# Turning x for the later batches on VectorE and through DRAM, unit-matrix transposes ahead of the first input, and a reordered end of the attention

## What is computed

```python
B, LQ, LK, D, H, HD = 4, 512, 512, 512, 16, 32
x = layer_norm(hidden_states, ln1_w, ln1_b)
q = (x @ q_w + q_b)                      # heads of 32
k = (encoder_hidden_states @ k_w + k_b)
v = (encoder_hidden_states @ v_w + v_b)
scores = where(mask, q k^T / sqrt(32), lowest)
out = softmax(scores) v
hidden = out @ cproj_w + cproj_b + hidden_states
y = layer_norm(hidden, ln2_w, ln2_b)
return hidden + gelu(y @ fc_w + fc_b) @ proj_w + proj_b   # inner width 2048
```

## Time and profile before

| | |
|---|---|
| median of 3 runs | 778.49 us (778.36 to 780.44) |
| profiled execution | 777.89 us, of which the span of the profile is 776.0 us |
| PE busy | 746.5 us, 96% |
| DVE, ACT, POOL busy | 468.8, 281.0, 276.9 us |
| projections | until about 152 us |
| attention | until about 410 us |
| MLP | until the end |

### The profile page before, as it was taken

The page is one execution under the profiler, slowest core; times in us unless marked ns, Lnnn a source line. Parts: engine busy times, 40 slices in busy tenths (PEclk is TensorE's granted clock), DMA queues, the critical chain, the costliest instruction groups (busy, mean ns, idle before and its releaser), DMA issues.

```text
span 776.0 us, 10021 instructions
## 1 busy us (share of the span) xinstructions
PE 746.5 (96%) x3664; PEld 514.7 (66%) x3664; DVE 468.8 (60%) x1012; ACT 281.0 (36%) x492; POOL 276.9 (36%) x166
## 2 busy tenths in 40 slices
PE   6999999889899999999979999999999999999998
PEld 5878886633334434444436888888888888888886
DVE  6673346889988899999768577533423343232213
ACT  3434241276766666667764011111112111211110
POOL 2654150066877677788644002113002200230000
PEclk9999999999999999999999999999999999999999
DMA  9656377587656785578640538240220404030001
GB/s 325 228 167 221 132 225 235 183 252 175 159 126 161 186 221 152 151 203 182 176 135 28 190 97 207 91 161 2 41 68 1 163 14 96 1 108 1 1 0 55
DMA packets 94384, 103.24 MB, mean 133 GB/s; under 512 B 39968, under 2 KB 48420, under 8 KB 94336
## 3 DMA queue, kind: packets, MB, share of 16 engines
q1 hardware_dynamic: 94192, 102.59, 45.5%
q10 hardware_dynamic: 144, 0.02, 0.0%
HBM read 73.08 MB, written 29.37 MB: 132 GB/s over the span
## 4 chain that ended last, share of the span: by engine, by line
PE 72%; DVE 19%; issue 3%; DMA 2%; ACT 2%; SPq 1%; POOL 0%; DVEq 0%; ACTq 0%
PE ps L481 20%; PE ps L483 20%; PE ps L482 20%; DVE ps L1001 10%; PE ps L604 3%; PE ps L573 3%; PE ps L588 3%; DVE R L1128 2%; PE ps L619 2%; DVE mx L1001 1%; PE ps L541 1%; DVE R L1022 1%; ACT Pt L790 1%; DMA RAWY<-in_q_w 1%; DVE R L937 1%
## 5 line engine op out<-in xcount | busy, mean ns | idle before, releaser
L790 ACT ACTIVATE Pt<-ps 128x512 f32<-128x512 f32 x256 | 137.4, 597 | 75.3 <-PE ps L588 74.1
L1175 DVE CAST HR<-R 128x512 fp32r<-128x512 f32 x52 | 24.3, 468 | 185.3 <-ACT R L825 185.3
L825 ACT ACTIVATE R<-ps,cols 128x512 f32<-128x512 f32 x52 | 35.9, 690 | 227.2 <-PE ps L483 227.1
L588 PE MATMUL ps<-BIG 98*128 98x512 f32 x256 | 93.4, 442 | 7.3 <-DVE R L1006 3.4
L1001 DVE CUSTOM_DVE_ANT_0 ps<-ps,FU 128x512 f32<-128x512 f32 x128 | 84.4, 720 | 14.5 <-PE ps L573 14.4
L588 PEld LDWEIGHTS ps<-BIG 98*128 98x128 f32 x256 | 44.8, 190 | 72.3 <-issue 24.6
L1001 DVE CUSTOM_DVE_ANT_0 ps<-ps,BIG 128x512 f32<-128x512 f32 x128 | 84.3, 720 | 7.6 <-PE ps L573 7.6
L481 PE MATMUL ps<-BIG,HR 128*128 128x512 f32 x192 | 74.8, 390 | 0.7 <-DVE HR L1177 0.7
L481 PE MATMUL ps<-YT,BIG 128*128 128x512 f32 x192 | 75.0, 390 | 0.0
L482 PE MATMUL ps<-YT,BIG 128*128 128x512 f32 x192 | 74.8, 389 | 0.0
L483 PE MATMUL ps<-BIG,HR 128*128 128x512 f32 x192 | 74.7, 389 | 0.0
(11 more groups left out here) (131 smaller groups left out, 1368.6 us busy)
## 6 DMA issues: line engine op xcount, KB each, us to landing
BIG<-qs SPq DMA_DIRECT2D x62, 256.0 KB, 2.7
BIG<-ks SPq DMA_DIRECT2D x62, 256.0 KB, 3.2
ks<-BIG SPq DMA_DIRECT2D x32, 256.0 KB, 2.1
qs<-BIG SPq DMA_DIRECT2D x32, 256.0 KB, 5.6
R<-hd SPq DMA_DIRECT2D x28, 256.0 KB, 4.4
R<-in_x SPq DMA_DIRECT2D x16, 256.0 KB, 5.5
hd<-R SPq DMA_DIRECT2D x16, 256.0 KB, 3.1
yt<-FU SPq DMA_DIRECT2D x64, 64.0 KB, 2.0
```

The lines of the kernel that those rows point to most:

```text
L588: eng.matmul(bk, K_[0:98, j, kc * 128:(kc + 1) * 128], Q_[0:98, j, :], start=True, stop=True).then_inc(S["p_ra"], 1)
L790: eng.activation(Pt[:, r, j % 2, :], bank(bank_a(("s2", i, j))), ACT.Exp, scale=SCALE).then_inc(S["a_ra"], 1)
L825: eng.activation(g, bank(4 + i % 2), ACT.Gelu_apprx_tanh, bias=fcb[:, f:f + 1]).then_inc(S["a_g"], 1)
L1175: eng.tensor_copy(HR[:, n, 0, :], g).then_inc(S["v_hh"], 1)
```

## The change

1. PE runs 16 transposes of the unit matrix by itself as soon as it is there, before its first projection. Nothing reads their result.
2. Only x of batch 0 is still turned by PE. For batches 1 to 3 DVE turns the normalized tile in 32x32 blocks (`x_block`, four STREAM_TRANSPOSE) into a buffer in the place of the high part of x, SP stores the blocks to `yt` in 16 DMAs of 64 KB in runs of 32 elements (`x_store`), loads them back in four DMAs (`x_load`) into R2, and `x_affine` works in place there and waits for the loads. The block transposes stand directly behind `x_norm`, ahead of the next group of low parts (L988) on DVE. On ACT `x_high(1)` stands behind the first V eviction of batch 1. On POOL the roots for batches 2 and 3 stand ahead of `x_low(1)` and behind `x_low(2)`. DMAs for raw x and for the leads wait for the block transposes instead of PE's.
3. At the end of the attention the affine, high and low parts of the second layer norm stand two items later, and `divide_c(12)` one item earlier, ahead of the pair adds.

```diff
-        Y_NORM, Y_BLOCKS, Y_AFFINE = (45, 47, 49, 51), (48, 49, 52, 53), (56, 56, 56, 56)
-        Y_HIGH, Y_LOW = (57, 57, 58, 58), (58, 58, 59, 59)
+        Y_NORM, Y_BLOCKS, Y_AFFINE = (45, 47, 49, 51), (48, 49, 52, 53), (58, 58, 58, 58)
+        Y_HIGH, Y_LOW = (59, 59, 60, 60), (60, 60, 61, 61)
...
+            def x_store(b):
+                dst = yt[b].rearrange("(k i) (c q j) -> c q i k j", i=32, q=4, j=32)
+                for c in range(4):
+                    sp.wait_ge("v_xb", 4 * (b - 1) + c + 1)
+                    for q in range(4):
+                        eng.dma_start(dst[c, q], blocks(b, c)[32 * q:32 * q + 32].rearrange(
+                            "i (k j) -> i k j", j=32)).then_inc(S[f"d_xs{c}"], 16)
+
+            def x_load(b):
+                sp.wait_ge("g_xl", 4 * b)
+                for c in range(4):
+                    sp.wait_ge(f"d_xs{c}", 64 * b)
+                for k in range(4):
+                    eng.dma_start(R2[:, k, :], yt[b, 128 * k:128 * k + 128]).then_inc(S[f"d_xl{k}"], 16)
...
             for b in range(B):
                 if b == 3:
                     load_stack(1)
+                if 0 < b < 3:
+                    x_store(b + 1)
                 for g in range(4):
                     store_qk(b, g, 0)
+                    if 0 < b < 3 and g == 1:
+                        x_load(b + 1)
...
                     load_raw(3, cv[2], 2)
+                    x_store(1)
...
                     if b == 0 and g == 1:
                         sp.wait_ge("g_lo", 3)
                         load_raw(0, xv[2], 2)
+                    if b == 0 and g == 2:
+                        x_load(1)
...
+            pe.wait_ge("cst", 2)
+            for n in range(16):
+                eng.transpose(bank(n % 4)[:, 0:128], ident[:, :], ident[:, :])
...
-                if 0 < b < 3:
-                    x_turn(b + 1)
...
-                    if b == 0 and g == 3:
-                        x_turn(1)
...
                     act.wait_ge("p_pj", 12 * b + c + 1)
                     eng.activation(V[:, 4 * b + c, :], bank(proj_bank(12 * b + c)), ACT.Copy).then_inc(S["a_v"], 1)
+                    if b == 1 and c == 0:
+                        x_high(1)
...
-                    if b == 0 and g == 3:
-                        x_high(1)
...
+            def x_block(b):
+                i = RAW_X[b][0]
+                if b >= 2:
+                    dve.wait_ge("p_pj", 12 * (b - 2) + 12)
+                for c in range(4):
+                    dve.wait_ge("v_nm", 4 * b + c + 1)
+                    eng.transpose(blocks(b, c), raw[i][:, c, :]).then_inc(S["v_xb"], 1)
...
-                    dve.wait_ge("p_tr", 4 * b + k + 1)
                     if b:
-                        dve.wait_ge("g_xl", 4 * (b - 1) + k + 1)
-                    eng.tensor_scalar(R2[:, k, :], bank(k), vec[:, 0, k:k + 1], vec[:, 1, k:k + 1],
+                        dve.wait_ge(f"d_xl{k}", 16 * b)
+                    else:
+                        dve.wait_ge("p_tr", k + 1)
+                    eng.tensor_scalar(R2[:, k, :], R2[:, k, :] if b else bank(k), vec[:, 0, k:k + 1], vec[:, 1, k:k + 1],
...
                     x_norm(b + 1)
+                    x_block(b + 1)
...
                     x_norm(1)
+                    x_block(1)
...
-                if kc == 2 and 2 <= s < NS - 1:
+                if i == 57 or (kc == 2 and 2 <= s < NS - 2):
                     divide_c(s - 2)
...
             root(1, 1)
             ctx_low(1)
+            root(0, 2)
             x_low(1)
```

More of the change, by code:

```diff
@@ L81, in cross_attention_block, with blocks @@
         MASK = [FU[:, 0, :], FU[:, 1, :], BIG[:, 2048:2560].bitcast(F32), BIG[:, 2560:3072].bitcast(F32)]
+        def blocks(b, c):
+            return BF[:, 12288 + 4096 * (b % 2) + 512 * c:12800 + 4096 * (b % 2) + 512 * c]
         def lead(s):
@@ L136, in cross_attention_block @@
                      "a_hi", "a_v", "a_qh", "a_qb", "a_nm", "a_xh", "a_ra", "a_pv", "a_ab", "a_ah", "a_wc", "a_g",
-                     "v_hi", "v_lo", "v_bn", "v_ag", "v_ve", "v_nm", "v_yb", "v_ya", "v_mf", "v_fu", "v_ql", "v_rb", "v_t1", "v_rc",
+                     "v_hi", "v_lo", "v_xb", "v_bn", "v_ag", "v_ve", "v_nm", "v_yb", "v_ya", "v_mf", "v_fu", "v_ql", "v_rb", "v_t1", "v_rc",
                      "v_t2", "a_sh", "v_at", "v_wc", "v_ac", "v_sh", "v_sl", "v_hh", "v_hl", "v_o", "v_cp",
@@ L141, in cross_attention_block @@
             S[name] = ctx.enter_context(nc.semaphore("s_" + name))
-        for name, n in (("d_st", 3), ("d_qk", 4), ("d_xr", 4), ("d_hd", 4), ("d_h", 4), ("d_hb", 4), ("d_o", 4), ("d_w", 2), ("d_hi", 2), ("d_mb", 4), ("d_ys", 4), ("d_yl", 4)):
+        for name, n in (("d_st", 3), ("d_qk", 4), ("d_xr", 4), ("d_hd", 4), ("d_h", 4), ("d_hb", 4), ("d_o", 4), ("d_w", 2), ("d_hi", 2), ("d_mb", 4), ("d_ys", 4), ("d_yl", 4), ("d_xs", 4), ("d_xl", 4)):
             for i in range(n):
@@ L289, in load_lead @@
                 if s < 2:
-                    sp.wait_ge("p_tr", 12)
+                    sp.wait_ge("v_xb", 8)
                 elif s < 4:
@@ L384, in _ @@
                     load_raw(1, cv[3], 2)
-                    sp.wait_ge("p_tr", 8)
+                    sp.wait_ge("v_xb", 4)
                     load_raw(2, xv[3], 2)
@@ L532, in proj_T, with x_turn @@
                     ins.then_inc(S["p_pj"], 1)
-            def x_turn(b):
-                pe.wait_ge("cst", 2)
-                pe.wait_ge("v_nm", 4 * (b + 1))
+            def x_turn():
+                pe.wait_ge("v_nm", 4)
                 for k in range(4):
-                    if b:
-                        pe.wait_ge("v_fu", 4 * (b - 1) + k + 1)
                     for c in range(4):
                         ins = eng.transpose(bank(k)[:, c * 128:(c + 1) * 128],
-                                            raw[RAW_X[b][0]][:, c, k * 128:(k + 1) * 128], ident[:, :])
+                                            raw[RAW_X[0][0]][:, c, k * 128:(k + 1) * 128], ident[:, :])
                     ins.then_inc(S["p_tr"], 1)
@@ L561, in ring_b @@
                 else:
-                    pe.wait_ge("v_fu", 13 + place)
+                    pe.wait_ge("v_fu", 1 + place)
                 return bank(bank_b(place))
@@ L673, in _ @@
                     if b == 0 and g == 2:
-                        x_turn(0)
+                        x_turn()
                     proj_T(b, g, 0)
@@ L1273, in _ @@
             ctx_low(1)
+            root(0, 2)
             x_low(1)
-            for b in (2, 3):
-                root(b % 2, b)
-                ctx_low(b)
-                x_low(b)
+            ctx_low(2)
+            x_low(2)
+            root(1, 3)
+            ctx_low(3)
+            x_low(3)
             for i in range(NI):
@@ L1299, in _ @@
                         if m == 0:
-                            pool.wait_ge("p_tr", 16)
+                            pool.wait_ge("v_xb", 12)
                         elif m == 1:
```

2 lines of the change are left out of this document (removed).

## The result

The changed kernel takes **796.8 us** (median of 4 runs, 795.0 to 799.4), the kernel before in the same comparison 779.5 (median of 4). The ratio is 1.0234, with an interval of 1.021 to 1.0259. That is 17.3 us slower; I had forecast 785.6, at most 793. The sign was right and the size was not. The profiled execution took 799.4 (span 797.6 against 776.0), so it lies 2.6 above its own median, and differences of single rows are read with that in mind.

The account below looks back on a forecast made before the run. PE was taken to bound the projections and the MLP. From the profiled 777.9 us, +1.7 for the unit transposes, +9.5 for the round trip and -3.5 for the attention's end gave 785.6; range 778.5 to 793.

Parts of the forecast that it names:

- Part 2: Projections, x of batches 1 to 3: the DRAM round trip outweighs the PE transposes saved; 9.5 us slower.
- 45.1 us from the first block (44.5) to the bank: Projections: x(1) and x(2) trips until DVE's low part of Q frees PE's bank for V of batch 2, at 89.6.
- +9.5: Projections: V of batch 2 9.5 us late, 1.7 saved by the third transpose group, 1.7 lost to the clock.
- Landing of x(1), 3.7 us after issue: Loads of turned x(1) from `yt`: last issued at 57.6, landed 3.7 us later, at 61.3.
- Stores of 7.8 us: SP's 16 block stores per batch: four took 1.95 in the quiet MLP, so sixteen take 7.8 us.
- Rival 3: Block stores fill the DMA queues, adding 8.5 us for one trip; total 794.1, chance 0.10.
- Normalizations of 5.0: DVE's four normalizations of x(2) beside POOL's low parts of x(1): 5.0 us, bounds 1.9 and 6.05.
- The second trip: x(2) through DRAM: first block at 71.6, stores until 79.4, loads landed at 86.4, affine done at 86.9.
- the third trip is hidden with 4 us to spare: x(3) through DRAM: bank for V of batch 3 free at 120, PE there at 124, so no wait.
- Part 1: gain 0, loss 1.7: Unit transposes before the first projection: V ends earlier, K still waits; the new 2.5 us stop costs 1.7 of clock.
- the case that I had as 783.9: Unit transposes don't raise the clock, so no stop arises before K; total 783.9, within the forecast's 0.60 chance.
- Part 3: -3.5: End of attention: 2.87 us stop and 1.7 of clock go, ACT's high parts cost 1.1; 3.5 us faster.

Follow-up runs that it names:

- The trip alone: Only x of batches 1 to 3 through DVE blocks and DRAM, on the kernel before; 796.3 us, ratio 1.0225.
- one batch ahead: Changed kernel with x(2) and x(3) turned a batch earlier, low parts of Q ahead of the blocks, raw x(2) and x(1)'s loads earlier; 781.5 us, ratio 1.0035.
- unit-only kernel: Only the 16 unit transposes ahead of the first projection, on the kernel before; 777.2 us, ratio 1.0001.
- two queues: Changed kernel with raw x(2) and x(1)'s loads issued earlier, plus half the block stores of x(1) and x(2) issued by ACT; 787.7 us, ratio 1.0101.
- lows first: Changed kernel with raw x(2) and x(1)'s loads issued earlier, plus DVE's low parts of Q of batch 0 ahead of x(1)'s blocks; 793.2 us, ratio 1.0195.
- loads first: Changed kernel with raw x(2) issued ahead of x(1)'s block stores and x(1)'s loads directly behind them; 789.4 us, ratio 1.0152.
- the version with the old end: Changed kernel with trips a batch earlier and leads ahead of the first stack, but the end of the attention put back; 778.6 us, ratio 0.999.

## Why the prediction was right or wrong

**Right: what decides.** Part 2 carries the loss; V of batch 2 waits for the chain x(1) to x(2) to ACT's high parts to the eviction of Q to DVE's low part; PE's earlier stops are inside it. The trip alone (796.3) shows the first, and the kernel with a stop taken away (no gain, and V of batch 2 as late as its blocks) the last.

**Wrong: the length of the chain.** I reckoned 45.1 us from the first block (44.5) to the bank; it took 54.2 (44.8 to 99.0). The mechanism was right, and the term +9.5 of the sum was sized too small. By its steps:

| step | forecast | measured |
|---|---|---|
| 16 stores of x(1) issued by | 52.3 | 53.3 |
| loads of x(1) issued, last landed | 56.3, 61.3 | 58.6, about 67 |
| affine of x(1) done | 61.8 | 67.6 |
| x(2) normalized | 65.9 to 70.9 | 71.6 to 77.4 |
| 16 stores of x(2) issued by | 79.4 | 86.9 |
| loads of x(2) issued, affine done | 81.4, 86.9 | 89.1, 96.8 |
| V of batch 2 | 89.6 | 99.0 |

- *Landing of x(1), 3.7 us after issue.* This is the largest single miss: 6.5 to 6.7, above even the 5.5 that I had as the slowest. Here raw x(2) and stores of Q were issued in the 5.3 us before and filled the engines (1.00 at 324 GB/s). Moving raw x(2) and the loads made the chain 5.7 us shorter. I had named "full queues" only as a rival for the *stores*, and looked for other traffic at 44 to 52, where there was none; it was at 56 to 68.
- *Stores of 7.8 us.* They took 8.5 and 8.9, the Q stores behind the first batch 2.9 instead of 2.0, and the four loads 2.7 to issue instead of 1.8. Rival 3 (4.08 for four) didn't come true: its sum, 794.1, was near the result for the wrong reason.
- *Normalizations of 5.0.* 5.8, beside POOL's four low parts of 5.6 in all. "SBUF — State Buffer" of the Trainium skill, in "SBUF: two separate sides", has GpSimd and VectorE, in a two-port mode, shut each other out for a whole instruction; the trace agrees, and also at 126.19, where DVE's affine took 6.44 beside POOL, against 2.0 for four alone (1.00 for two).
- *The second trip.* It repeats the small misses: 1.1 in the stores, and 2.2 in landing and affine. The affine waited 1.42 between its second and third quarter, and its last two took 1.89 instead of 1.0, beside POOL.
- *A small slip.* From the first block store to the first affine's end the forecast's own numbers make 16.0, not 15.9.

**Wrong: that the third trip is hidden with 4 us to spare.** PE stood 1.14 for it (134.81). Raw x(3) landed at 106.7, 12.7 later than I had it, where the chain behind x(2) was only 9.4 late, and the affine took the 6.44 beside POOL.

**Missing: the leads.** The block stores are moved in front of the K stores, the stack and the leads on SP, and I followed SP only to the loads of x. PE stood 1.79 us for the leads in the kernel after, and 5.0 in the version with the trips ahead; a low clock followed in both. In that version it was the rest of the loss: 781.5 to 774.9.

**Part 1: gain 0, loss 1.7.** The gain was right. The loss is there in one profile of ten. In the kernel after the clock rose only at 10.56, so no stop arose (the case that I had as 783.9); where it rose at once, one stop of six brought a low clock.

**Part 3: -3.5.** By the medians it is -3.1 alone, clear of zero, and about that again with the trips hidden, where the intervals just overlap. So the size was right, but not for a reason that the record shows, which makes it luck. The term rested on one row of one execution, and the three other profiles with the old end don't have that stop.

**The sum with measured terms:** 18.2 for the trip, 0 for the unit transposes and -3.1 for the end make 15.1 over before, against 17.3 measured; the intervals, 2 to 4 us each way for a kernel of 4 runs, cover the difference. My +9.5 was worth 18.2.

**What the trip can bring at all.** PE saves three groups of transposes and a stop, 5.9 us. One batch ahead and with the leads first, the trips bring the first exponential 2.6 earlier (149.78), 3.1 with the old end (149.32) and 0.5 without the unit transposes (151.95). With the old end the whole is at 0.999 [0.9968, 1.0011]: nothing that can be told. "VectorE: DVE Perf Modes" of the Trainium skill, in "Rules for kernel authors", advises TensorE for a 128x128 turn where PSUM will do as the target. The runs agree as the change stands (+18.2), and with the best order found they show no gain against it. The two fastest kernels are the one before with the new end alone (775.1, ratio 0.996) and the one with all three parts, the trips one batch ahead and the leads first (774.9, ratio 0.995). They can't be told apart, and the first is the smaller change.

## What to carry to other kernels

Price a load from issue to landing by what has been issued in the microseconds before it, not by a row of the same load in a quiet stretch: 3.0 to 4.9 us became 6.6 behind 1 MB and a few stores, and everything behind it in the chain came later by that. When DMAs are put on a queue, follow *all* that stands behind them to the first thing that PE waits for; here it was four small loads 50 us later. And a round trip through DRAM must start a whole stage ahead: the same instructions cost 18 us in a chain of two, and nothing that can be told one batch earlier and with the leads moved ahead.

## What the runs showed of the hardware

- Sixteen transposes of the unit matrix from 1.53 took 3.68 us, the pace of the lower level, in both kinds of execution. In the unit-only kernel V then ran at the upper level from 5.79; in the kernel after its matmuls stood 0.43 apart until 10.56, as without the transposes (until 10.7 in the kernel without them). Six of ten profiles were of the first kind. The same instructions didn't raise the clock each time; why is open.
- Pieces of 128 bytes, stored from one queue, move at 113 to 130 GB/s with the DMA engines some 0.7 busy. From two queues the engines are full, at 177 to 205 GB/s, against 324 to 346 GB/s for other traffic at 0.90 to 1.00. The issue of 16 stores goes from 8.5 to 5.5 us, but the wait for them only from 10.0 to 8.0.
- Stops of PE of 3.9 us and more were followed by the low clock every time (0.57, 0.50 and 0.57 in the rows above). Between 1.8 and 2.9 us both happened. Behind 1.79 (142.31), 1.98 (one batch ahead), 2.00 (lows first), 2.18 (two queues) and 2.87 the clock was low; behind 1.79 (80.58), 1.93 (unit transposes alone), 2.53 (one batch ahead) and 2.70 (loads first) it was not.
- The clock is low without any such stop too: in the attention of the end-alone kernel it was 0.57 from 212 to 224 us with no wait over 0.53 before. The executions of one kernel spread over some 8 us (773.1 to 781.5 for the version with the old end), and the mean granted clock goes with it (0.998 and 0.990 for these two; 0.008 of 778 us is 6.2). So a single profile against another doesn't show a difference under 4 us, and the ratios of 10 to 12 runs are good to 1.4 to 2.6 us each way.
